# Moving the second job of a VectorE cycle behind the additions, in a four-layer transformer kernel

## The reference, cut to what matters

```python
x = x + _L0_attn_ref(_layernorm(x, axis=-1), ...)   # 16 heads, no mask
x = x + _L0_ffn_ref(_layernorm(x, axis=-1), ...)
x = x + _L1_attn_ref(_layernorm(x, axis=-1), ...)   # 16 heads, causal
x = x + _L1_ffn_ref(_layernorm(x, axis=-1), ...)
x = x + _L2_attn_ref(_layernorm(x, axis=-1), ...)
x = x + _L2_ffn_ref(_layernorm(x, axis=-1), ...)
x = x + _L3_attn_ref(_layernorm(x, axis=-1), ...)   # 16 heads, region mask and per-key bias
x = x + _L3_ffn_ref(_layernorm(x, axis=-1), ...)
```

## Time and profile before

| what | value |
|---|---|
| median of 3 runs | 3919.72 us (3916.33 to 3926.92) |
| the profiled execution | 3920.88 us, span 3919.2 us |
| TensorE matmul busy | 3633.6 us, 93% of the span |
| VectorE busy | 2901.8 us, 74% |
| ScalarE busy | 2270.1 us, 58% |
| GpSimd busy | 196.1 us, 5% |
| additions L1242 | 1152 instructions, 1353.5 us, 1175 ns each on average |
| low parts L1177 of Q | 96 instructions, 750 ns; idle before them 167.8 us, ended by ACT Qh L972 |
| low parts L1177 of K | 96 instructions, 751 ns; idle before them 157.8 us, ended by ACT Kh L972 |

### The profile page before, as it was taken

The page is one execution under the profiler, slowest core; times in us unless marked ns, Lnnn a source line. Parts: engine busy times, 40 slices in busy tenths (PEclk is TensorE's granted clock), DMA queues, the critical chain, the costliest instruction groups (busy, mean ns, idle before and its releaser), DMA issues.

```text
span 3919.2 us, 65392 instructions
## 1 busy us (share of the span) xinstructions
PE 3633.6 (93%) x24661; PEld 1907.6 (49%) x24661; DVE 2901.8 (74%) x5821; ACT 2270.1 (58%) x2635; POOL 196.1 (5%) x273
## 2 busy tenths in 40 slices
PE   4999999999999958999999996699999999999997
PEld 2455455454554424555555554245545455554544
DVE  5777878778787777777777765477777877778784
ACT  3666666666666516655655652466666666666663
POOL 1000000000000001212222210000000000000000
PEclk9999999999999989999999997899999999999998
DMA  1000000000000000000000000000000000000000
GB/s 51 7 9 10 9 11 8 9 10 9 9 7 7 9 13 7 15 15 12 15 12 13 10 15 3 19 7 12 7 9 10 10 9 10 9 10 8 7 10 17
DMA packets 44398, 44.27 MB, mean 11 GB/s; under 512 B 16466, under 2 KB 30554, under 8 KB 43834
## 3 DMA queue, kind: packets, MB, share of 16 engines
q1 hardware_dynamic: 44090, 40.09, 3.3%
HBM read 37.56 MB, written 1.70 MB: 10 GB/s over the span
## 4 chain that ended last, share of the span: by engine, by line
PE 79%; DVE 11%; issue 4%; ACT 3%; DMA 1%; SPq 1%; POOL 0%; DVEq 0%; ACTq 0%
PE ps L565 76%; DVE over L1264 2%; DVE acc L1242 2%; DVE wexp L1264 1%; DVE x L1402 1%; ACT Kh L972 1%; ACT work L1000 1%; PE ps L863 1%; PE ps L874 1%; DVE stats L1150 1%; DVE Kd L1181 1%; PE ps L554 1%; SPq L475 0%; PE ps L903 0%; DMA auxQ<-mrow 0%
## 5 line engine op out<-in xcount | busy, mean ns | idle before, releaser
L1000 ACT ACTIVATE work<-ps 128x1024 f32<-128x1024 f32 (+1 forms) x1344 | 1276.8, 994 | 950.6 <-PE ps L565 943.9
L1242 DVE TENSOR_TENSOR acc<-acc,work 128x1024 f32<-128x1024 f32 (+2 forms) x1152 | 1353.5, 1175 | 49.4 <-ACT work L1000 11.8
L565 PE MATMUL ps<-work,V 128*64 128x512 f32 (+3 forms) x5376 | 1239.9, 581 | 0.0
L565 PEld LDWEIGHTS ps<-work,V 128*64 128x64 f32 x5376 | 452.8, 138 | 547.2 <-issue 452.7
L565 PE MATMUL ps<-Qh,Kh 64*128 64x512 f32 (+3 forms) x2688 | 654.2, 482 | 32.4 <-issue 10.8
L1264 DVE CUSTOM_DVE_ANT_0 over<-ps,over,mpart 128x512 f32<-128x512 f32 (+3 forms) x642 | 422.3, 695 | 310.4 <-PE ps L565 310.2
L565 PE MATMUL ps<-Qh,Kl 64*128 64x512 f32 (+3 forms) x2688 | 525.7, 385 | 0.0
L565 PE MATMUL ps<-Ql,Kh 64*128 64x512 f32 (+3 forms) x2688 | 522.5, 383 | 0.0
L565 PE MATMUL ps<-auxQ,auxK 64*128 64x512 bf16 (+3 forms) x2688 | 518.6, 380 | 0.0
L1264 DVE CUSTOM_DVE_ANT_0 wexp<-ps,wexp 128x512 f32<-128x512 f32 (+1 forms) x632 | 376.5, 635 | 24.1 <-PE ps L565 19.2
L565 PE MATMUL ps<-Kh,Qh 64*128 64x512 f32 (+2 forms) x1520 | 343.1, 464 | 35.8 <-DVE mpart L1264 14.5
(11 more groups left out here) (188 smaller groups left out, 2599.3 us busy)
## 6 DMA issues: line engine op xcount, KB each, us to landing
rden<-inverse_sums SPq DMA_DIRECT2D x192, 128.0 KB, 2.8
auxQ<-mrow SPq DMA_DIRECT2D x384, 1.0 KB
wqk<-in_wqk SPq DMA_DIRECT2D x24, 128.0 KB, 2.5
dcomp<-rden SPq DMA_DIRECT2D x192, 2.0 KB
wv<-in_wv SPq DMA_DIRECT2D x24, 64.0 KB, 2.3
inverse_sums<-rcomp SPq DMA_DIRECT2D x96, 4.0 KB, 1.3
work<-in_mlp_w SPq DMA_DIRECT2D x1, 1024.0 KB
work<-in_c_aux SPq DMA_DIRECT2D x1, 1024.0 KB, 4.9
```

Of the source, the lines that this page charges most:

```text
L565: return pe.matmul(o, w, m, start=start, stop=stop, skip_group_check=True)
L1000: act.activation(work[:, 2 * e:2 * e + 2, q0:CH], ps[:, b:b + 2, q0:CH], ACT.Exp, scale=L.scale).then_inc(s["p_ready"], 1)
L1242: dve.tensor_tensor(o, o, work[:, slots[two]:slots[two] + 2, q0:CH], ALU.add).then_inc(s["acc_ready"], 1)
```

## The change

In VectorE's `cycle`, the call `jobs(1)` moves down: it stood behind the first two additions, and now it stands behind all of them but the last, which belongs to the next cycle.

```diff
                     for which in sums[:1]:
                         add(*which)
                     jobs(0)
-                    for which in sums[1:2]:
+                    for which in sums[1:-1]:
                         add(*which)
                     jobs(1)
-                    for which in sums[2:-1]:
-                        add(*which)
                     jobs(2)
```

## The result

| | before | after |
|---|---|---|
| median | 3919.17 us (8 runs, 3911.76 to 3926.92) | 3899.89 us (8 runs, 3892.1 to 3905.65) |
| ratio | | 0.9939, 95% interval 0.9919 to 0.9958 |
| profiled execution | 3920.88 us, span 3919.2 | 3900.25 us, span 3898.5 |
| mean granted clock of TensorE | 0.972 | 0.974 |

The kernel became 0.6% faster: the forecast direction, but more than the 0.40% forecast. So the surplus over the forecast is some 3 to 4 us, and one comparison by itself hardly tells it from none.

The account below looks back on a forecast made before the run. TensorE was taken to bound the kernel (79% of the chain), with waits for `mcol`. Gains of 14.4 + 1.4 = 15.8 us off 3920.88 gave 3905.1, less 1.2 for the runs' median, rounded 3904 us; range 3897 to 3914 us.

Parts of the forecast that it names:

- What bounds the kernel, and where: TensorE makes 79% of the chain; in the first attention it waits 15 times, 5.3 us in all, for `mcol`.
- Does the addition fit: Two additions, 2.45 us, fit into the 2.54 us before the job, which starts on time with 0.09 us spare.
- The heads: First and third attentions, cycle starts (to the matmul behind `excess`) at g = 3, 4, 7, 8 shorten: 14.4 us less.
- The causal order: In the causal attention, at g = 0, the earlier addition gains 0.2 us per pair, 1.4 us in all.
- rival D: Causal attention: 1.2 GHz stretches fall differently, up to 17 us either way; 3898 or 3910 us; small shifts within forecast's 0.66.
- A: In the heads, `exp` of the second tile or a late job gives part back; 3910 to 3913 us; chance 0.22.
- B: No gain: another wait, for instance `base`, ends at the same time as `mcol`; 3917 to 3921 us; chance 0.06.
- C: Slower: job late behind a waiting addition (causal g = 0, 2, or g = 3, 7); about 3932 us; chance 0.02.

Follow-up runs that it names:

- e5: The kernel before with the job moved the other way, behind the first addition only, in all three attentions: 4010.5 us, ratio 1.0229.
- e1: The kernel before with the job moved in the first and third attention only, causal order kept: 3911.2 us, ratio 0.9979.
- e2: The kernel before with the job moved in the causal attention only (14 places): 3909.9 us, ratio 0.9979.
- e10: The kernel before, unchanged, run once more with a second profile: 3924.2 us, ratio 1.0002 to before.
- e8: The changed kernel with two matmuls of V's third chunk made twice per causal pair, restoring its length: 3910.2 us, 0.9968 of the kernel before.
- e3: The kernel before with the addition moved ahead of K jobs only (28 places, first and third attention): 3908.8 us, ratio 0.9971.
- e9: The changed kernel, run once more with a second profile: 3903.1 us, ratio 0.9951 to the kernel before.
- e4: The kernel before with the projection of Q's first chunk computed twice in each causal pair: 3919.8 us, ratio 0.9997.

## Why the prediction was right or wrong, point by point

- **What bounds the kernel, and where**: right. The 15 waits for `mcol` were the handle; one is left in the first attention and one or two in the third, as the window is drawn. e5 shows the same mechanism from the other side.
- **Does the addition fit**: right. The job starts 2.54 us behind the second addition as before. The pair of additions behind each other takes 2.53 us to its end, which leaves no idle time to see; I had left 0.09 us between 2.45 and 2.54. At the other moved places of the two attentions (g = 2 and 6) 0.14 us of idle time are left.
- **The heads**: right in mechanism and nearly in size, 14.4 us forecast, 13.1 us in the trace and 13.6 +- 1.2 us by e1 at the same clock. The shares also hold: g = 4 went to 5.05 us (forecast 5.05), g = 7 to 4.96, g = 8 to 5.03. What lacks is mostly the waits for the DMA into `auxQ` named above, which the prediction had not seen coming.
- **The causal order**: 1.4 us forecast, 7 x 0.2 us in the trace (8.87 to 8.67 us at g = 1), 3.7 +- 1.2 us by e2 at the same clock. GpSimd's busy time is 23.5 us in most causal pairs after and 23.5 to 24.3 before, so no cost of a new meeting with it shows.
- **The step that failed** is rival D: the clock in the causal attention got no term in the sum, only a little width. I had priced it about rightly (34 us at half clock, up to 17 us; the 12 stretches cost 12 x 1.55 = 19 us), but I took it for a matter of luck and of a start that comes 7 us sooner. The start came only 0.5 us sooner, since the part between the attentions took 6 us longer, and before kept its 12 stretches when it started 5.8 us later (e10). What the runs showed in its place is that the clock also goes with the length of the causal pair. e1 keeps the pair: 10 stretches in its profile, and no higher clock than before. e2 changes nothing but the causal order, which shortens the pair by 0.2 us: one stretch in its profile, and 0.0028 more mean clock. e8 restores the pair's length and takes the 0.0026 away again. Why a pair of this length brings the stretches back, and why e1's clock is below before's, stays open. The missing term, by the mean clocks of before and after, is 0.0018 x 2.3 / 0.001 = 4 us, and what is left of the measured 19.3 us beside the 13.1 and 1.4 us of the trace is 4.8. By the two pairs of profiles it is (15.5 + 6.0) / 2 - 1.4 = 9 us, but two profiles of each are few, and the time between the attentions differs by 8 us between before's own two. The Trainium skill (TensorE: Matmul & The Clock Gate, What's actually happening) says that the point of the transition varies from run to run. The traces agree for the changed kernel (3 and 9 stretches); the kernel before had 12 in the same cycles twice, but its causal order had 10 and 6 in e1 and e3. I had drawn from it that the time would scatter and not shift. It does both.
- **The range** ended at the upper bound of the heads and the causal order alone, 3897 us, and the chance for more was put at 0.04. Since D could shift the time by more than a few microseconds and its sign was not known, the lower end belonged some 5 to 9 us deeper. That the measured time fell just outside the range and not just inside is chance: e9 would have lain inside.
- **Rivals A, B and C** did not come as such: the heads reach their floor, TensorE waits for `Kl` or `Ql` in the first and third attention no more than before (once, 0.2 us), and g = 9 to 15 kept their lengths. The little that was given back (some 1 us) went to a DMA and not, as A had it, to `exp` or a late job.

## What to carry to other kernels

Work that an in-order engine does behind a job that it has to wait for is paid for twice. Put it ahead of the job if its inputs are old, and count the result by the moment at which the next consumer's input is ready, down to the floor that a cycle without the wait shows. And look at the granted clock of each repetition of a loop, not at its mean: a loop whose repetitions all dip at the same place is paying a price that, here, a small change in its length lifted and brought back, and a comparison of two kernels should say how much of it is the clock's.

## What the runs showed of the hardware that I had not expected

- A stretch at 1.2 GHz behind the waits for the maxima of g = 2 or 9 (about 2 us together) cost 1.55 us of the causal pair, and in the kernel before both returned in each of six pairs, 109.2 us apart, in two profiles of two. The head of g = 4, with 0.54 us of such waits, never had one. With the new order, 0.2 us shorter, six pairs in a row had none in e2, four of six in the first profile of the changed kernel, and none of six was free of them in its second.
- Adding 0.22 us of matmuls per pair (e8) cost 7 us in all, and adding 0.87 us per pair (e4) cost nothing that could be measured.
- The spread of some 10 us between executions of one kernel goes nearly all with the mean clock: 2.3 us for 0.001 of it, with 1.8 us left over.
